# Query evacuations moved to ScalarE; in all batches but the last, the output rows and the transposed reciprocals are copied out of PSUM by ScalarE and added and multiplied by GpSimd

## What is computed

```python
# layer 1, x: (4, 2048, 256)
q, k, v = split((x @ w_in.T + b_in).reshape(b, l, 16, 48))
att = softmax(einsum('blhd,bmhd->blmh', q, k) * 0.25, axis=2)
opt = einsum('blmh,blhd->blhd', att, v).reshape(b, l, d)
x = layernorm(x + opt @ w_out.T + b_out)
# layer 2
dist = softmax(mean(x @ Wr + br, axis=1)); idx = sort(top_k(dist, 4))
Qs, Ks, Vs = the chosen heads of x @ Wq + bq, x @ Wk + bk, x @ Wv + bv
score = softmax(Qs @ Ks.T / 8)
out = layernorm(x + (score @ Vs) @ Wo + bo)
```

## Time and profile before

| | |
|---|---|
| median of 3 runs | 3705.18 us (3704.74 to 3706.42) |
| the profiled execution's own time | 3707.26 us |
| its span in the trace | 3705.5 us |
| busy: PE, DVE, ACT, POOL | 93%, 92%, 76%, 48% of the span |
| instructions | 45,135 |
| mean granted TensorE clock | 0.981 of full speed |

### The profile page before, as it was taken

One profiled execution on the slowest core, in us unless ns is written; L12 is line 12 of the kernel. 1 busy time (PEld: TensorE's weight loads), 2 busy tenths in 40 slices (PEclk: granted clock), 3 DMA queues, 4 the chain that ended last, 5 costly groups with the idle time before them and its releaser, 6 DMA issues. The chain is left out here.

```text
span 3705.5 us, 45135 instructions
## 1 busy us (share of the span) xinstructions
PE 3433.0 (93%) x14464; PEld 1298.0 (35%) x14464; DVE 3400.8 (92%) x5376; ACT 2812.5 (76%) x3033; POOL 1788.8 (48%) x1251
## 2 busy tenths in 40 slices
PE   8989998889999999899999999899999999899998
PEld 3334433432232324343232324343232324343333
DVE  7999999999999999889999999989999999467776
ACT  5998898778888888688888888688888887333333
POOL 4344333304444446455444446455444446758775
PEclk9999999899999999899999999899999999999999
DMA  5222222200010001200010101200000000100000
GB/s 166 80 90 93 76 83 68 83 22 18 18 29 18 29 18 41 76 16 22 18 29 18 29 18 46 70 18 21 18 29 18 29 18 18 50 1 12 12 12 12
DMA packets 117215, 142.84 MB, mean 39 GB/s; under 512 B 33394, under 2 KB 100466, under 8 KB 116978
## 3 DMA queue, kind: packets, MB, share of 16 engines
q1 hardware_dynamic: 116978, 139.95, 12.4%
HBM read 89.55 MB, written 50.33 MB: 38 GB/s over the span
## 5 line engine op out<-in xcount | busy, mean ns | idle before, releaser
L1130 ACT ACTIVATE scores<-scores,nmax 128x2048 f32<-128x2048 f32 x1024 | 2042.0, 1995 | 315.5 <-DVE scores L1321 304.4
L985 PE MATMUL ps<-stack 96*128 96x512 bf16 x4792 | 1299.9, 388 | 122.0 <-DVE scores L1321 94.9
L894 POOL TENSOR_TENSOR facc<-facc,probs 128x1024 f32<-128x1024 f32 x443 | 1049.3, 2369 | 598.1 <-ACT probs L1240 530.2
L1321 DVE TENSOR_SCALAR_CACHE_REDUCE scores<-ps,lows 128x1024 f32<-128x1024 f32 x1024 | 1278.8, 1278 | 34.3 <-PE ps L985 28.2
L1321 DVE TENSOR_SCALAR_CACHE_REDUCE scores<-ps 128x1024 f32<-128x1024 f32 x1024 | 1216.9, 1217 | 25.6 <-PE ps L985 24.4
L985 PEld LDWEIGHTS ps<-stack 96*128 96x128 bf16 x4792 | 372.7, 99 | 1168.6 <-DVE scores L1321 658.9
L1380 DVE TENSOR_REDUCE smax<-ps 128x2 f32<-128x1024 f32 x512 | 621.0, 1220 | 123.0 <-PE ps L1050 121.9
L1050 PE MATMUL ps<-fk,fq 64*128 64x512 f32 x2048 | 564.2, 632 | 60.6 <-DVE smax L1380 46.1
L1065 PE MATMUL ps<-fq,fk 64*128 64x512 f32 x2048 | 546.2, 611 | 10.6 <-DVE smax L1380 4.8
L1085 PE MATMUL ps<-probs,vals 128*64 128x512 f32 x2048 | 532.3, 615 | 4.8 <-DVE oT L1428 4.8
L1240 ACT ACTIVATE probs<-ps 128x1024 f32<-128x1024 f32 x384 | 385.4, 1012 | 88.1 <-PE ps L1068 87.7
(11 more groups left out here) (129 smaller groups left out, 2175.9 us busy)
## 6 DMA issues: line engine op xcount, KB each, us to landing
stack<-qk_levels SPq DMA_DIRECT2D x768, 64.0 KB, 2.2
qk_levels<-fk SPq DMA_DIRECT2D x64, 384.0 KB, 2.4
probs<-in_L_attn_x SPq DMA_DIRECT2D x16, 512.0 KB, 4.1
v_rows<-vals SPq DMA_DIRECT2D x16, 512.0 KB, 2.9
vrows<-v_rows SPq DMA_DIRECT2D x16, 512.0 KB, 3.3
res<-in_L_attn_x SPq DMA_DIRECT2D x16, 512.0 KB, 4.0
x_rows<-y SPq DMA_DIRECT2D x16, 512.0 KB, 2.9
res<-x_rows SPq DMA_DIRECT2D x16, 512.0 KB, 3.9
```

What stands on the lines that cost most here:

```text
L894: pool.tensor_tensor(total, total, probs[:, slot, :], ALU.add).then_inc(facc_ready, 1)
L985: last = pe.matmul(bank(banks[i]), stack[0:SK, hd % 2, 0, t * P:(t + 1) * P], stack[0:SK, hd % 2, 1, col:col + CH], start=True, stop=True)
L1130: act.activation(row, row, ACT.Exp, bias=nmax[:, k % LOWS:k % LOWS + 1], scale=-1.0, accum_out=esum[:, b % 2, t, hd:hd + 1]).then_inc(exp_ ...
L1321: dve.tensor_scalar(scores[:, k % ROW_SLOTS, half * TILE:(half + 1) * TILE].rearrange("p (a n) -> p a n", a=2), two_banks(banks), 1.0, fir ...
```

## The change

Three evacuations of PSUM leave DVE. ACT now evacuates QP with `activation(Identity)`, whose bias is scaled beforehand (one small instruction more on DVE at the start). In batches 0 to 2, R becomes a plain copy by ACT and a multiplication in SBUF by POOL. In batches 0 to 2, OP and FO become two copies by ACT of 128 x 512 into `y`, one addition by POOL of 128 x 1024 (the new unit YA), and then the row statistics on DVE, which now wait for YA. In the last batch R, OP and FO stay as they were. The load of the next residual rows (LR) waits for YA in place of the DVE unit.

```diff
-        for kind, eng in (("QP", dve), ("KP", act)):
+        for kind, eng in (("QP", act), ("KP", act)):
...
-            unit(eng(*t), 0.75, [pe(*t)] + ([was("LV", *two)] if i >= 2 else []))
+            unit(eng(*t), 0.6, [pe(*t)] + ([was("LV", *two)] if i >= 2 else []))
...
-            unit(dve("R", b, g), 0.68, [pe("R", b, g), last] + free)
+            if b + 1 < B:
+                unit(act("R", b, g), 0.5, [pe("R", b, g), pe("V", b, g, STEPS - 1)] + free)
+                unit(pool("R", b, g), 1.25, [act("R", b, g), last])
+            else:
+                unit(dve("R", b, g), 0.68, [pe("R", b, g), last] + ([pool("R", *one)] if g == 0 else []))
...
+        if b + 1 < B:
+            unit(act(k + "h", b, c), 0.5, [pe("part", 1, *t)] + free)
+            unit(act(*t), 0.5, [pe(*t), act(k + "h", b, c)])
+            unit(pool("YA", *t), 2.46, [act(*t), pool("RB", *t)])
+            unit(dve(*t), 1.8, [pool("YA", *t)] + ([dve(*norms[i - 1])] if i else []))
+        else:
+            unit(dve(k + "h", b, c), 1.45, [pe("part", 1, *t), pool("RB", *t), dve(*norms[i - 1])] + free)
+            unit(dve(*t), 1.75, [pe(*t), dve(k + "h", b, c)])
...
+                elif kind == "YA":
+                    i = norm_no[at]
+                    pool.wait_ge(res_ready, i + 1)
+                    pool.wait_ge(y_half, i + 1)
+                    pool.wait_ge(y_ready, i + 1)
+                    pool.tensor_tensor(y[:, i % 2, :, :], y[:, i % 2, :, :], res[:, i % 2, :, :], ALU.add).then_inc(y_added, 1)
...
+                elif kind == "R":
+                    b, g = at
+                    pair, c = g % PAIRS, g // PAIRS
+                    pool.wait_ge(r_copied, group_no(b, g) + 1)
+                    pool.wait_ge(oacc_ready, sum_no(b, g, BURSTS - 1))
+                    pool.tensor_tensor(foT(c)[:, pair, :], foT(c)[:, pair, :], oacc[:, g % 2, :], ALU.mult
+                                       ).then_inc(foT_ready, 1)
...
+                    act.activation(q32[:, i % 2, :], bank(banks[0]), ACT.Identity, bias=qk_bias[:, at[1]:at[1] + 1],
+                                   scale=-float(AD) ** -0.5).then_inc(q32_ready, 1)
...
+                    rows = y[:, i % 2, 2 * half:2 * half + 2, :].rearrange("p t d -> p (t d)")
+                    act.activation(rows, bank(banks[half]), ACT.Copy).then_inc(y_ready if half else y_half, 1)
...
+                    act.activation(foT(c)[:, pair, :], bank(banks[0]), ACT.Copy).then_inc(r_copied, 1)
...
+                elif moved:
+                    dve.wait_ge(y_added, nth["POOL", "YA", *n[1:]])
+                    for half in range(2):
+                        row_stats(norm_no[n[1:]], half)
```

More of the change, by code:

```diff
@@ L331, in plan @@
                 if q == 0:
-                    free = [dve("R", *two)] if two else []
+                    free = [r_done(*two)] if two else []
                 else:
@@ L352, in plan @@
         old = norms[i - 2] if i >= 2 else None
-        unit(sp("LR", *t), 0.6, late + ([dve(*old)] if old else [pe("A", 0, HEAD_TILES)]), 3.0)
+        unit(sp("LR", *t), 0.6, late + ([y_done(*old)] if old else [pe("A", 0, HEAD_TILES)]), 3.0)
         unit(pool("RB", *t), 2.4, [sp("LR", *t)])
-        fill(t, 3.75, 2, [act("OT", b, c)] if k == "OP" else [dve("R", b, PAIRS * c + p) for p in range(PAIRS)], dve(*t))
+        fill(t, 3.75, 2, [act("OT", b, c)] if k == "OP" else [r_done(b, PAIRS * c + p) for p in range(PAIRS)], (act if b + 1 < B else dve)(*t))
         free = []
@@ L622, in build @@
         inputs_done = max(last_user.values())
-        halves = [n[2:] for n in order["DVE"] if n[1] == "QP"]
+        halves = [n[2:] for n in order["ACT"] if n[1] == "QP"]
         half_no = {t: i for i, t in enumerate(halves)}
@@ L975, in _ @@
                     else:
-                        pe.wait_ge(read_by[was[:2]], nth[was])
+                        pe.wait_ge(read_by[was[:2]], group_no(*was[2:]) + 1 if was[:2] == ("DVE", "R") else nth[was])
                 if kind == "A":
@@ L1272, in _, with row_stats @@
             dve.wait_ge(wT_ready, KC + 2)
-            dve.tensor_copy(qk_bias[:, :], ps[:, 3, 0:4]).then_inc(wT_read, 1)
+            dve.tensor_scalar(qk_bias[:, 0:2], ps[:, 3, 0:2], -float(AD) ** -0.5, None, ALU.mult)
+            dve.tensor_copy(qk_bias[:, 2:4], ps[:, 3, 2:4]).then_inc(wT_read, 1)
             dve.tensor_copy(heads(bv_rows[:, :]), parts[:, 2, :, :]).then_inc(wT_read, 1)
             dve.wait_ge(wT_read, 5)
+            def row_stats(i, half):
+                s = i % 2
+                for r in (2 * half, 2 * half + 1):
+                    last = dve.bn_stats(st[:, s, r, :], y[:, s, r, :])
+                last.then_inc(bn_ready, 1)
+                if half:
+                    dve.wait_ge(bn_ready, i * BN_STEPS + 2)
+                    for r in range(TPC):
+                        last = dve.bn_aggr(mv[:, s, r, :], st[:, s, r, :])
+                    last.then_inc(bn_ready, 1)
             def add_rows(t, half, into):
@@ L1290, in add_rows @@
                 dve.wait_ge(added, i + 1)
[L1291 to L1298 removed]
+                row_stats(i, half)
             logits, probs_r = route[:, 0:NR], route[:, NR:2 * NR]
@@ L1306, in _ @@
                 banks = held.get(("PE", "T" if kind == "C" else kind[:2]) + at)
-                if banks and kind != "M":
+                moved = kind in ("OP", "FO") and at[0] + 1 < B
+                if banks and kind != "M" and not moved:
                     dve.wait_ge(filled, fill_no[("T",) + at if kind == "C" else n[1:]])
```

70 lines of the change are left out of this document (43 added, 27 removed).

## The result

The changed kernel takes 3678.4 us (median of 4 runs, 3677.9 to 3679.63), the kernel before 3705.8 us (4 runs, 3704.74 to 3706.84): 27.4 us less, a ratio of 0.9927 with a 95% interval of 0.9911 to 0.9942. The profiled execution took 3678.28 us with a span of 3676.2 us. The forecast was 3673.9 us.

A forecast was written before the change was run, and what follows sets the result against it. DVE was taken to set the pace in stage one and the middles, PE behind seams. Terms -17.2 - 21.9 + 2.4 - 3 + 2.7 + 3.5 + 2.2 = -31.3 us gave 3673.9 us; range 3650 to 3697.

The forecast's parts named there:

- QP: Stage one: 26 evacuations in the DVE-bound stretch leave DVE at 0.66 us each, -17.2 us.
- the new wait: DVE's statistics wait for POOL's addition 24 times, 0.1 us each: +2.4 us, bounds 0 and 57.
- R in the middles: DVE-bound stretches of batches 1 to 3: R leaves DVE, 10.95 us of the 21.9 us gain.
- FO in the middles: DVE-bound stretches of batches 1 to 3: FO's additions leave DVE, 10.95 us of the 21.9 us gain.
- the seams and the order: Later first S, partly given back: -3, +2.7, +3.5 us for batches 0 to 2, +2.2 in batch 3's seam.
- ACT did not take over: Rival for stage one: ACT at 96% lets DVE wait and the 17.2 us are lost; 3691 us, chance 0.06.
- PE was the bound all along: No-change rival, whole kernel: PE at 93% bounds and DVE only follows; 3705 us, chance 0.07.
- POOL's new work comes back on DVE's tiles: Rival: POOL's 48 new instructions hold DVE up for all of the 21.9 us; 3696 us, chance 0.07.
- The slower rival: DVE's statistics stand before a late POOL; slower from 1.4 us a wait, up to 3728 us, chance 0.07.
- that rule: GpSimd shares an SBUF read port with DVE, so the 21.9 us might return as waits; not for tiles, which read PSUM.
- POOL is full in the seams: Rival: POOL's added work in the seams brings X1 18 us late, +22 in two seams; 3696 us, chance 0.11.

The follow-up runs named there:

- e1: Kernel before with only the QP evacuations moved to ACT; R and the additions of OP and FO stay on DVE: 3688.73 us, -19.9.
- e2: Kernel before with only the 24 R of batches 0 to 2 moved, copied by ACT and multiplied by POOL: 3685.79 us, -22.9.
- e10: Kernel before with the order of all engines planned as for e2, but R itself put back on DVE: 3695.63 us, -12.5.
- e9: Changed kernel with OP's additions and FO's of chunks 2 and 3 back on DVE; QP, R and FO of chunks 0 and 1 moved: 3654.68 us, -53.5.
- e5: Changed kernel with all additions of OP and FO back on DVE; QP and R stay moved: 3665.57 us, -46.2.
- e4: Kernel before with DVE doing each R of batches 0 to 2 twice, first into a spare buffer, order unchanged: 3718.25 us, +9.6.
- e8: Changed kernel with FO's additions back on DVE; QP, R and OP's additions stay moved: 3684.56 us, -27.2.
- e3: Kernel before with only the additions of OP and FO of batches 0 to 2 moved to ACT copies and POOL sums: 3705.11 us, -3.6.
- e12: Changed kernel with POOL's sum cut to the first column of each residual row, same order and waits: 3672.35 us, -35.8.

## Why the prediction was right, and by which steps it was not

By parts of the run, with the forecast's terms for the middles and the new wait spread evenly over the three batches, the sum came out like this (us):

| part | forecast | changed less before |
|---|---|---|
| to the first J | -17.2 | -21.8 |
| batch 0 | -7.3 + 0.8 - 3 = -9.5 | -9.4 |
| batch 1 | -7.3 + 0.8 + 2.7 = -3.8 | -1.3 |
| batch 2 | -7.3 + 0.8 + 3.5 = -3.0 | -3.3 |
| from J of batch 3 | +2.2 | +6.6 |

By the experiments the change is made of these terms:

| step of the prediction | forecast | measured |
|---|---|---|
| QP | -17.2 | -19.9 (e1) |
| R in the middles | -10.95 (16 of 24) | -10.4 (e2 less e10, all 24) |
| FO in the middles, with the new wait | -10.95 + 2.4 | -7.3 (e9 less e5; 12 of the 16 additions) |
| the seams and the order | -3 + 2.7 + 3.5 + 2.2 = +5.4 | order -12.5 (e10); OP and FO of chunks 2 and 3: +26.1 (changed less e9); not additive, -3.4 |
| sum | -31.3 | -27.4 |

The measured column adds up because each term is the difference between two runs of one chain; the sizes of the single terms are less sure than their sum.

**QP** held: DVE paces stage one. Its busy time there fell by 20.0 us (583.05 in the 587.6 us up to the first J before) and the stretch by 21.8. ACT did not take over: no wait of DVE for its exponentials stands in stage one, at 95.4% where I had 96%. Some of the 2.7 us above the forecast may be PE's clock, whose grant in stage one was 0.98 before and 1.00 after. At 0.99 in both, the stretch from 60 us to the first J is 585.3 us in e2 and 569.4 in e5, a difference of 15.9. Whether the higher grant came with the change was not tried apart.

**R and FO in the middles** held in size: the three cycles of e9, which moves all R and 12 of the 16 additions of the middles, are 6.8, 7.7 and 6.4 us shorter than those of e10, 20.9 us for 24.6 us of DVE. The forecast had 21.9. In e2 against e10 the price was near full in the middles of batches 0 and 1, nothing in that of batch 2, and about 0.6 us for each microsecond of DVE over all 24 R, a third of which lie outside the middles. The rival that PE was the bound all along is out (e1, e4), though PE's grant still moves a middle. So is the rival that POOL's new work comes back on DVE's tiles: the R and the six sums that e9 gives POOL gained most of what they take from DVE.

**The new wait** was 4.5 us in two places, both in seam 1, for 2.4 forecast. The slower rival, 1.4 us at each of 24 statistics, did not come near.

**The seams** are the step that failed, twice and with opposite signs. I priced them by when the first S starts and by the additions that left DVE. That much held. The first S of batches 0, 1 and 2 comes 14.1, 5.4 and 5.4 us later behind the first J than before, where I had 13.4, 7.0 and 8.7. What is given back is as I had it too: in e8, where S comes 16 to 21 us later than in e5, batch 0 loses nothing, as at DVE's pace, and batches 1 and 2 lose 9.0 and 10.7 us, nearer to PE's. What failed is, first, that the new order gains by itself (-12.5 us in e10), which I had at nothing, and second, that the moved additions lose about 26 us against the order that e9 makes; of that 11.1 us lie behind the J of batch 3, which I had at 2.2.

For the order's gain, left out was that DVE's last NM in the seam depends on what POOL does beside it. In the seam of the earlier trace rows it took 9.4 us from line 788 on. POOL in that place of the kernel before:

```profile
1515.64 7.35 POOL L894 TENSOR_TENSOR facc<-facc,probs 128x1024 f32<-128x1024 f32 x3
1522.96 2.33 POOL L849 TENSOR_TENSOR res<-res,bo_rows 128x1024 f32<-128x1024 f32 x1
1525.25 1.25 POOL L900 TENSOR_TENSOR oacc<-oacc,part 128x512 f32<-128x512 f32 x1
1526.47 2.33 POOL L849 TENSOR_TENSOR res<-res,bo_rows 128x1024 f32<-128x1024 f32 x1
```

DVE's three slow instructions there (line 792 is in the earlier trace rows):

```profile
1523.05 2.27 DVE L794 TENSOR_SCALAR newt<-newt 128x4 f32<-128x4 f32 x1
1525.35 1.18 DVE L796 TENSOR_TENSOR rstd<-rstd,newt 128x4 f32<-128x4 f32 x1
```

Each ends as POOL's instruction ends: 1520.79 + 2.23 = 1523.02 with POOL's 1522.99, 1525.32 with 1525.29, 1526.53 with 1526.50. In the order of e2 the same NM meets POOL's own NM, which is of another form, and passes (POOL, then DVE):

```profile
1504.88 4.94 POOL L824 TENSOR_SCALAR y<-y,mv,rstd 128x256 f32<-128x256 f32 x4
```

```profile
1506.39 0.27 DVE L819 TENSOR_SCALAR newt<-newt 128x4 f32<-128x4 f32 x1
1506.70 0.16 DVE L821 TENSOR_TENSOR rstd<-rstd,newt 128x4 f32<-128x4 f32 x1
1506.89 1.84 DVE L824 TENSOR_SCALAR y<-y,mv,rstd 128x256 f32<-128x256 f32 x4
```

From 1505.89 to 1508.73 that is 2.84 us instead of 9.41, on the chain to X1. How much of the order's gain this makes is not shown, since no run changed it alone: in e10 the first S of batch 1 comes 122 us behind the first J instead of 134, while the whole cycle is 1.9 us shorter. In e3 that NM is as short (2.97 us), without a gain that can be told from nothing. The Trainium skill (Perfetto Trace Analysis, Optimizing Scalar/DVE Operations) warns of the read port that GpSimd shares with DVE; the trace agrees for NM, whose operands lie in SBUF, and the tiles showed nothing of it. I had weighed that rule for the tiles and dropped it; it applied to the seam.

The changed kernel has the short NM too (from 1497.01 to 1499.77, beside POOL's NM), and loses elsewhere: the projections of the seam go through ACT and POOL before DVE can take the statistics, POOL has its NM and softmax sums in the same place, and DVE stands without a tile. In the cycle of batch 1, from its first J to its first M, DVE waits 21.2 us for tiles and 4.5 for POOL's sum, in e9 12.8 and 0 (the changed kernel, then e9):

```profile
DVE scores L1391 <- PE ps L1018: 21.2, 17, 4.6
DVE st L1343 <- POOL y L878: 4.5, 2, 2.4
```

```profile
DVE scores L1401 <- PE ps L1025: 12.8, 24, 3.3
```

e12 puts 6 to 8 us of the whole loss on POOL's sum. In seam 3 DVE is held up as in the NM above: the twelve scaling instructions of DVE's three NM there take 14.3 us before, 19.4 in the changed kernel and 14.7 in e9 (the group of line 819 of the changed kernel, then that of line 824 of e9):

```profile
L819 DVE TENSOR_SCALAR y<-y,mv,rstd 128x256 f32<-128x256 f32 x12 | 19.4, 1676 | 0.1
```

```profile
L824 DVE TENSOR_SCALAR y<-y,mv,rstd 128x256 f32<-128x256 f32 x12 | 14.7, 1287 | 0.1
```

How the rest of the 26 us divides into order, banks and waits was not taken apart, so the cause of this loss stays open. That the total came out within 4.5 us is in part luck: a gain of 12.5 us that I had not seen paid for half of a loss of 26 us, for which I had all seams together at 5.4. Of the rivals "POOL is full in the seams" had the place but not the size. In the seam of batch 1 the last NM of POOL ends 80.7 us after AT of chunk 1, where the rival had 87 and more, but the last X1 comes 85.8 us after that AT, 6.5 later than before instead of 18.

## What to carry to other kernels

Where lists are planned, moving one operation changes the order of everything: run the new order with the old assignment (e10) before the gain is put down to the engine that was relieved. Move work off the bounding engine where that engine bounds, and leave it in stretches where a chain decides; here the kernels with a hop more in the chain (copy, sum, statistics) lost more in the seams than the same move gained in the middles, and keeping it out of the seams made the best kernel (3654.68 us). Compare whole cycles, not stretches, between two orders.

## What the runs showed of the hardware

- A DVE instruction on 128 x 4 numbers in SBUF lasted until POOL's TENSOR_TENSOR in progress ended (2.23, 2.27 and 1.18 us instead of 0.16 to 0.17), while POOL's TENSOR_SCALAR beside it cost it next to nothing (0.16 to 0.27 us, also where both of its inputs lie in SBUF; four scalings of 128 x 256 took 1.84 us, and 1.38 in the earlier trace rows).
- The same kernel differs from run to run with PE's granted clock: of the ten runs of the kernel before in the last set, 3702.95 us came at 0.983 and 3716.72 us at 0.979. Its first three runs, 1.7 us apart, had made it look steadier. With the same DVE list up to the first J, e2 reached it at 645.3 us (grant 0.99) and e10 at 650.2 us (0.97).
